# Software-pipelining the context quantization (phase D) and splitting the output rows (phase E) of a BitNet transformer layer on eight cores

## The chip, the cores and the metric

The kernel runs on the 8 cores of one Trainium2 chip, with the same program on every core and no communication between them. The metric is the device time of the slowest core in microseconds. Cores 0 to 3 form one die, 4 to 7 the other.

## The reference, cut to what matters

The input x is 4 x 4096 x 2048 in float32. The layer returns the input plus an attention branch plus a gated FFN branch, both fed with a layer-normalized x. All four projections of the attention are "bitlinear": ternary weights, and activations rounded to 8 bits with one scale for each token.

```python
def bitlinear(x, W):
    sw = jnp.mean(jnp.abs(W)) + 1e-05
    Wq = jnp.clip(jnp.round(W / sw), -1.0, 1.0) * sw
    sx = 127.0 / jnp.clip(jnp.max(jnp.abs(x), axis=-1, keepdims=True), 1e-05, None)
    xq = jnp.clip(jnp.round(x * sx), -128.0, 127.0) / sx
    return jnp.einsum('bsd,od->bso', xq, Wq)
...
p = jax.nn.softmax(scores, axis=-1)
out = jnp.einsum('bkgst,bktd->bkgsd', p, v)
out = out.transpose(...).reshape(b, s, D_MODEL)
return bitlinear(out, Wo)
...
x = x + attn(layernorm(x)) + ffn(layernorm(x))
```

The change touches the last two steps: the rounding of the attention's output (`out`, the context) ahead of `Wo`, and the product with `Wo` with the two additions.

## The kernel before, in words

A core owns 2048 tokens of one batch entry and goes through six parts, one after the other: the FFN for its tokens (its result goes to a DRAM scratch, `ffn_scr`), keys and values, queries, attention (phase C), **phase D**, the context's quantization, and **phase E**, the output projection. A `phase_fence` between parts makes every engine wait until PE, DVE and ACT have finished the part before.

Each `E(engine, fn, waits, inc)` appends one step to an engine's own program. Every engine runs its list in order. The waits are semaphore counts: `ve`, `pe` and `ac` count the steps of VectorE, TensorE and ScalarE, so a wait on `(ve, ve.n)` is a wait for the last VectorE step written so far, whatever it was. The order of the work is thus the order in which the code is written.

**Phase D** (L821 to L873) handles 16 tiles of 128 tokens, all in one chain of dependences. Attention left the context as `ctxT`, feature on the partitions. For a tile: TensorE transposes 8 blocks into a bank of the PSUM tile `d_ptr` and VectorE copies it to `ctok` (L840, L844), twice; VectorE multiplies by the inverse softmax sums into the float32 tile `d_cn` (L852), takes the row maximum (L855), and forms the scale and its inverse in two short steps (L858, L861); ScalarE scales and adds a large constant (L863) and subtracts it again with an integer output `d_ci` (L866), which rounds; VectorE casts to bf16 `d_cq` (L868); and `emit_tr16` (L190) transposes back in two groups of 8 through the same two banks of `d_ptr` (L198), each copied to `cqT` by VectorE (L202). Both kinds of transposes wait on `(ve, ve.n)`, and there is one `d_cn`, so one tile's chain ends before the next one's begins.

**Phase E** (L877 to L935) first quantizes `Wo` (`emit_wquant`: every weight chunk is loaded twice by SP's queue), and then for each of 16 token tiles SP's queue loads the 1 MB row block `e_x` of x (L896), POOL's queue loads the 1 MB block `e_f` of `ffn_scr` (L903), TensorE makes four groups of 16 matmuls of 512 columns (L910), alternating between two PSUM tiles `e_po`, ScalarE writes each group scaled into a quarter of `e_o` (L915), VectorE adds `e_x` (L920) and then `e_f` (L922) over all 2048 columns, and SP's queue stores the 1 MB block (L925). `e_x`, `e_f` and `e_o` have two buffers each. A load into a buffer waits for the additions two tiles earlier; but SP issues in order, so the load of `e_x` for a tile also stands behind the store of the tile before it. The program ends when the last stores have landed.

Of the kernel before, what the change touches and what calls it, by code (L numbers as in the profile page):

```python
# [44 lines left out]
def build_program():  # L45
# [49 lines left out]
    s_ost = [sem("s_ost0"), sem("s_ost1")]  # L95
# [724 lines left out]
    def phase_d():  # L820
        dstack = ExitStack()  # L821
        with dstack:
            ctok = sb("d_ctok", [128, D], BF16, dstack)
            cn = sb("d_cn", [128, D], F32, dstack)
            cm = cn
# [10 lines left out]
            for tt in range(16):  # L836
                for g in range(2):
# [23 lines left out]
                E("vector", lambda e, tt=tt: e.reciprocal(sx[:], rsxo[:, tt:tt + 1]),  # L861
                  waits=[(ve, ve.n)], inc=(ve, 1))
                E("scalar", lambda e: e.activation(cm[:], cn[:], AF.Identity,  # L863
                                                   scale=sx[:, 0:1], bias=bC1),
                  waits=[(ve, ve.n), (ac, ac.n)], inc=(ac, 1))
# [13 lines left out]
    def phase_e():  # L879
        estack = ExitStack()  # L880
        with estack:
# [10 lines left out]
            orow_st = [0, 0]  # L892
            efence = [(ve, ve.n), (ac, ac.n), (pe, pe.n)]
            for tt in range(16):
# [12 lines left out]
                for oc in range(4):  # L907
                    pb = oc % 2
                    E("tensor", lambda e, tt=tt, oc=oc, pb=pb: [
# [5 lines left out]
                    E("scalar", lambda e, tt=tt, oc=oc, pb=pb, tb=tb: e.activation(  # L915
                        orow[tb][:, oc * 512:(oc + 1) * 512], po[pb][:],
                        AF.Identity, scale=rsxo[:, tt:tt + 1]),
                      waits=[(pe, pe.n), (ac, ac.n), (s_ost[tb], orow_st[tb])], inc=(ac, 1))
# [9 lines left out]
                orow_st[tb] = s_ost[tb].n  # L928
            E("sync", None, waits=[(s_ost[0], s_ost[0].n), (s_ost[1], s_ost[1].n)])
# [118 lines left out]
```

How the kernel before makes its waits and increments, by code:

```python
            def _run(eng):  # L937
                for waits, fn, inc in prog.ops[name]:
                    for (s, v) in waits:
                        eng.wait_ge(s.h, v)
                    if fn is None:
                        continue
                    ins = fn(eng)
                    if inc is not None:
                        ins.then_inc(inc[0].h, inc[1])
```

## Time and profile before

| what | us |
|---|---|
| median of 2 runs (5829.81 and 5950.91) | 5890.36 |
| the profiled execution's own time | 5866.16 |
| its span, slowest core (core 6), first to last instruction | 5864.6 |
| span of the fastest core (core 3) | 5784.6 |
| granted TensorE clock, cores 0 to 3 / 4 to 7 | 0.848 / 0.841 |

The profile is one execution; start times count from the first instruction of core 6. A timeline row gives the start, the duration, the engine, the line, output <- input, and in brackets how long the engine was idle before and what released it. PE is TensorE, PEld its weight load, DVE is VectorE, ACT is ScalarE, POOL is GpSimd and SP is SyncE; SPq is a DMA issued by SP. A granted clock of 1.0 is 2.4 GHz and 0.5 is 1.2 GHz.

### The profile page before, as it was taken

What the parts mean: (1) busy time and instruction counts of PE and PEld (TensorE: products, weight loads), DVE (VectorE), ACT (ScalarE), POOL (GpSimd) and SP (SyncE); (2) the same over time, 40 slices, a digit from 0 to 9 for tenths busy, and PEclk for the clock granted to TensorE, in tenths of its full rate; (3) what the DMA queues carried; (4) which work ended last, traced back from release to release, by engine and by line L of the source; (5) the groups of instructions that cost most, each with busy time, mean ns of one, the idle gap of its engine ahead of it and who ended that gap; (6) DMA issues with size and microseconds to landing.
All of it is one profiled execution on the core that took longest, in us unless ns stands there. A gap on an engine that the chain in (4) does not pass through costs nothing.

```text
span 5864.6 us, 54466 instructions; the slowest of 8 cores (5784.6 to 5864.6 us)
## 1 busy us (share of the span) xinstructions
PE 3912.3 (67%) x18728; PEld 1781.8 (30%) x18728; DVE 1676.7 (29%) x2621; ACT 1638.0 (28%) x1375; POOL 303.0 (5%) x276
## 2 busy tenths in 40 slices
PE   1899978889998885244542044456889889922059
PEld 1344434434443442122331033342222222211024
DVE  4100000000000001455554365564322111144433
ACT  4111100011111001333330522213556656612131
POOL 0111110011111000000000000000000000000000
PEclk9999999999987997576776577789999999955579
DMA  3688877767766675311114501111000000000655
GB/s 117 65 79 75 77 69 81 81 72 72 72 63 63 72 84 101 111 58 49 51 49 115 147 31 44 44 33 46 11 9 8 7 5 6 4 0 0 165 194 215
DMA packets 793288, 387.59 MB, mean 66 GB/s; under 512 B 551488, under 2 KB 777152, under 8 KB 778688
## 3 DMA queue, kind: packets, MB, share of 16 engines
q0 software_dynamic: 548608, 161.50, 26.4%
q1 hardware_dynamic: 244416, 222.61, 12.9%
q8 instruction: 161, 2.64, 0.2%
q14 instruction: 103, 0.84, 0.1%
HBM read 480.53 MB, written 41.94 MB: 89 GB/s over the span
## 4 chain that ended last, share of the span: by engine, by line
PE 57%; DVE 18%; ACT 10%; DMA 9%; issue 5%; DVEq 1%; ACTq 0%; SPq 0%; POOL 0%; POOLq 0%
PE f_pd_h L341 11%; PE f_pg_h L300 11%; PE f_pu_h L306 11%; PE e_po L910 4%; PE c_pse L736 3%; PE c_ppv L740 3%; ACT c_pp L794 2%; DMA wo_wb<-wo_t 2%; PE c_psc L785 2%; DMA wq_wb<-wq_t 2%; PE c_psc L783 2%; PE c_pse L738 2%; PE c_ppv L742 2%; PE b_pkv L554 2%; DVE b_mx L165 2%
## 5 line engine op out<-in xcount | busy, mean ns | idle before, releaser
L794 ACT ACTIVATE c_pp<-c_psc 128x1024 bf16<-128x1024 f32 x640 | 655.4, 1024 | 581.4 <-PE c_psc L785 581.4
L300 PE MATMUL f_pg_h<-xnT,f_gw_h 128*128 128x512 bf16 x2816 | 655.1, 393 | 34.4 <-DMA f_uw_h<-uw_t 34.4
L341 PE MATMUL f_pd_h<-hdnT,f_dw_h 128*128 128x512 bf16 x2816 | 641.9, 391 | 44.5 <-DMA f_dw_h<-dw_t 44.5
L306 PE MATMUL f_pu_h<-xnT,f_uw_h 128*128 128x512 bf16 x2816 | 652.1, 392 | 0.0
L651 PE MATMUL b_pq<-b_xqT,qtern 128*128 128x256 bf16 x2048 | 270.3, 292 | 267.4 <-DVE b_qrot L660 258.7
L803 DVE TENSOR_TENSOR c_pp<-c_pp,cmask 128x512 bf16<-128x512 bf16 x512 | 217.8, 425 | 797.9 <-ACT c_pp L794 768.8
L321 DVE TENSOR_TENSOR hdnT<-f_sg_h,f_su_h 128x1024 bf16<-128x1024 bf16 x88 | 60.9, 693 | 1254.6 <-ACT f_su_h L317 1254.6
L341 PEld LDWEIGHTS f_pd_h<-hdnT,f_dw_h 128*128 128x128 bf16 x2816 | 283.9, 101 | 392.9 <-issue 83.3
L300 PEld LDWEIGHTS f_pg_h<-xnT,f_gw_h 128*128 128x128 bf16 x2816 | 282.8, 101 | 392.4 <-issue 133.3
L306 PEld LDWEIGHTS f_pu_h<-xnT,f_uw_h 128*128 128x128 bf16 x2816 | 282.6, 100 | 354.7 <-issue 97.2
L532 PE MATMUL b_pkv<-b_xqT,ktern 128*128 128x256 bf16 x1024 | 178.8, 357 | 288.4 <-DVE b_krot L541 271.5
L736 PE MATMUL c_pse<-c_pp,c_onehot 128*16 128x512 bf16 x640 | 244.8, 383 | 134.4 <-DVE c_pp L803 129.7
L651 PEld LDWEIGHTS b_pq<-b_xqT,qtern 128*128 128x128 bf16 x2048 | 206.2, 104 | 331.5 <-issue 295.2
L198 PE MATMUL b_ptr<-c_identbf,b_xq 128*128 128x128 bf16 x768 | 79.6, 286 | 327.9 <-DVE b_xq L187 327.9
L910 PE MATMUL e_po<-otern,cqT 128*128 128x512 bf16 x1024 | 224.0, 382 | 96.7 <-DVE otern L441 96.7
L358 DVE COPY f_ffs_h<-f_ptf_h 128x512 f32<-128x512 f32 x64 | 44.3, 692 | 766.8 <-PE f_ptf_h L354 766.8
L783 PE MATMUL c_psc<-c_qh,kT 128*128 128x512 bf16 x640 | 244.7, 382 | 21.3 <-DMA c_qh<-q_scr 21.3
L313 ACT ACTIVATE f_sg_h<-f_pg_h,c_gs 128x1024 bf16<-128x1024 f32 x88 | 98.1, 1115 | 557.6 <-PE f_pg_h L300 557.6
L740 PE MATMUL c_ppv<-c_pp,vT 128*128 128x512 bf16 x640 | 250.6, 392 | 0.0
L347 ACT ACTIVATE f_fft_h<-f_pd_h,c_ds 128x1024 f32<-128x1024 f32 x32 | 35.7, 1114 | 769.2 <-PE f_pd_h L341 769.2
L317 ACT ACTIVATE f_su_h<-f_pu_h,c_us 128x1024 bf16<-128x1024 f32 x88 | 98.1, 1115 | 538.2 <-PE f_pu_h L306 538.2
L785 PE MATMUL c_psc<-c_qh,kT 128*128 128x512 bf16 x640 | 245.0, 383 | 0.0
(163 smaller groups left out, 3996.8 us busy)
## 6 DMA issues: line engine op xcount, KB each, us to landing
f_gw_h<-gw_t POOLq DMA_DIRECT2D x88, 512.0 KB, 8.1
f_uw_h<-uw_t POOLq DMA_DIRECT2D x88, 512.0 KB, 10.1
f_dw_h<-dw_t POOLq DMA_DIRECT2D x32, 1408.0 KB, 18.0
b_xch<-x_kv SPq DMA_DIRECT2D x16, 2048.0 KB, 7.8
wq_wb<-wq_t SPq DMA_DIRECT2D x32, 1024.0 KB, 6.8
wo_wb<-wo_t SPq DMA_DIRECT2D x32, 1024.0 KB, 7.3
f_xch<-x_q SPq DMA_DIRECT2D x4, 4096.0 KB, 17.2
ffn_scr<-f_ffs_h SPq DMA_DIRECT2D x32, 512.0 KB, 11.3
```

The lines of the kernel that those rows point to most:

```text
L300: e.matmul(pg[:, bi, tc * 512:(tc + 1) * 512], gwb[bi][:, dt, :], xnT[:, dt, half * HT + tc * 512: half * HT + (tc + 1) * 512], start=(dt ...
L306: e.matmul(pu[:, bi, tc * 512:(tc + 1) * 512], uwb[bi][:, dt, :], xnT[:, dt, half * HT + tc * 512: half * HT + (tc + 1) * 512], start=(dt ...
L341: e.matmul(pd[:, bi, tc * 512:(tc + 1) * 512], dwb[bi][:, it, :], hdnT[:, it, tc * 512:(tc + 1) * 512], start=(it == 0), stop=(it == NIT - 1))
L532: e.matmul(pkv[pb][:, 0:256], ktern[:, dt, kv * 128:(kv + 1) * 128], xqT[:, cb, dt, :], start=(dt == 0), stop=(dt == NDT - 1))
L651: e.matmul(pq[pb][:], qtern[:, dt, h * 128:(h + 1) * 128], xqT[:, 0, dt, :], start=(dt == 0), stop=(dt == NDT - 1))
L736: e.matmul(pse[:], c_onehot[:, 16 * h:16 * h + 16], pp[:, k0 % 8, :], start=fse, stop=False),
L740: e.matmul(ppv[h % 2][:], vT[:, k0, kvh * 128:(kvh + 1) * 128], pp[:, k0 % 8, :], start=fpv, stop=False),
L783: e.matmul(psc[sbk][:, 0:512], kT[:, kvh, k0 * 128:(k0 + 1) * 128], qh[hb][:], start=True, stop=True),
L785: e.matmul(psc[sbk][:, 512:1024], kT[:, kvh, k1 * 128:(k1 + 1) * 128], qh[hb][:], start=True, stop=True)][-1],
L794: E("scalar", lambda e, k0=k0, sbk=sbk: e.activation(pp[:, (k0 % 8):(k0 % 8) + 2, :].rearrange("p a b -> p (a b)"), psc[sbk][:], AF.Exp, s ...
L803: E("vector", lambda e, k=k, mi=mi: e.tensor_mul(pp[:, k % 8, :], pp[:, k % 8, :], cmask[:, mi, :]), waits=[(ac, ac.n), MASKOK, (ve, ve.n) ...
L910: e.matmul(po[pb][:], cqT[:, dt, tt * 128:(tt + 1) * 128], otern[:, dt, oc * 512:(oc + 1) * 512], start=(dt == 0), stop=(dt == NDT - 1))
```

## The change

In phase D the loop body is cut into four functions. `stage_a` is the transposes, the copies to `ctok` and the multiplication; `stage_b` the maximum and the scales; `stage_c` the two ScalarE steps; `stage_d` the cast, the transposes back and the copies to `cqT`. The code writes `stage_c(tt)`, `stage_a(tt+1)`, `stage_b(tt+1)`, `stage_d(tt)`. `d_cn` and the inverse scale get two buffers, the transposes back get two PSUM banks of their own (`d_ptr2`), and the waits name the step that is really needed instead of the last one written, except for `stage_c`, which still waits on `(ve, ve.n)`: when it is written, that is the last copy of `stage_d(tt-1)`. In phase E the two additions and the store are done for each quarter of 512 columns, right behind the ScalarE step that made it, each quarter with its own store semaphore.

```diff
@@ phase_d
-            cn = sb("d_cn", [128, D], F32, dstack)
-            cm = cn
+            cn = sb("d_cn", [128, 2, D], F32, dstack)
...
-            sx = sb("d_sx", [128, 1], F32, dstack)
+            sx = sb("d_sx", [128, 2], F32, dstack)
...
+            ptr2 = ps("d_ptr2", [128, 2, 1024], BF16, dstack)
...
+            aptr_ve = [ve.n, ve.n]
+            cptr_ve = [ve.n, ve.n]
+            cn_ac = [ac.n, ac.n]
+            cq_ve = [ve.n]
+            p2_ac = [ac.n] * 16
+
+            def stage_a(tt):
+                tp = tt % 2
                 for g in range(2):
...
-                      waits=[(ve, ve.n)], inc=(pe, 1))
+                      waits=[(ve, aptr_ve[g])], inc=(pe, 1))
                     E("vector", lambda e, g=g, bank=bank: e.tensor_copy(
                         ctok[:, g * 1024:(g + 1) * 1024], bank[:]),
                       waits=[(pe, pe.n), (ve, ve.n)], inc=(ve, 1))
-
-                def bc_mul(e, tt=tt):
+                    aptr_ve[g] = ve.n
+
+                def bc_mul(e, tt=tt, tp=tp):
...
-                E("vector", bc_mul, waits=[(ve, ve.n), RSEOK], inc=(ve, 1))
...
+                E("vector", bc_mul, waits=[(ve, ve.n), RSEOK, (ac, cn_ac[tp])], inc=(ve, 1))
+
+            def stage_b(tt):
...
+            def stage_c(tt):
+                tp = tt % 2
+                E("scalar", lambda e, tp=tp: e.activation(cn[:, tp, :], cn[:, tp, :], AF.Identity,
+                                                          scale=sx[:, tp:tp + 1], bias=bC1),
                   waits=[(ve, ve.n), (ac, ac.n)], inc=(ac, 1))
...
+                  waits=[(ac, ac.n), (ve, cq_ve[0])], inc=(ac, 1))
+                cn_ac[tp] = ac.n
+                p2_ac[tt] = ac.n
+
+            def stage_d(tt):
                 E("vector", lambda e: e.tensor_scalar(cq[:], ci[:], 1.0, None, ALU.mult),
-                  waits=[(ac, ac.n), (pe, pe.n)], inc=(ve, 1))
+                  waits=[(ac, p2_ac[tt]), (pe, pipe_pe[0])], inc=(ve, 1))
...
-                          ptr, rdy, tt)
+                          ptr2, rdy, tt, cptr_ve)
+                pipe_pe[0] = pe.n
+
+            pipe_pe = [pe.n]
+            stage_a(0)
+            stage_b(0)
+            for tt in range(16):
+                stage_c(tt)
+                if tt + 1 < 16:
+                    stage_a(tt + 1)
+                    stage_b(tt + 1)
+                stage_d(tt)
@@ phase_e
...
-                      waits=[(pe, pe.n), (ac, ac.n), (s_ost[tb], orow_st[tb])], inc=(ac, 1))
+                      waits=[(pe, pe.n), (ac, ac.n), (s_ost[tb][oc], ost_oc[tb][oc])], inc=(ac, 1))
                     po_ac[pb] = ac.n
-                E("vector", lambda e, tb=tb: e.tensor_add(orow[tb][:], orow[tb][:], xrow[tb][:]),
-                  waits=[(ac, ac.n), XOK, (ve, ve.n)], inc=(ve, 1))
-                E("vector", lambda e, tb=tb: e.tensor_add(orow[tb][:], orow[tb][:], frow[tb][:]),
-                  waits=[(ve, ve.n), FROK], inc=(ve, 1))
+                    E("vector", lambda e, tb=tb, sl=sl: e.tensor_add(
+                        orow[tb][:, sl], orow[tb][:, sl], xrow[tb][:, sl]),
+                      waits=[(ac, ac.n), XOK, (ve, ve.n)], inc=(ve, 1))
+                    E("vector", lambda e, tb=tb, sl=sl: e.tensor_add(
+                        orow[tb][:, sl], orow[tb][:, sl], frow[tb][:, sl]),
+                      waits=[(ve, ve.n), FROK], inc=(ve, 1))
+                    E("sync", lambda e, tt=tt, tb=tb, sl=sl: e.dma_start(
+                        out=out[tt * 128:(tt + 1) * 128, sl], in_=orow[tb][:, sl]),
+                      waits=[(ve, ve.n)], inc=(s_ost[tb][oc], 16))
+                    ost_oc[tb][oc] = s_ost[tb][oc].n
                 row_ve[tb] = ve.n
-                E("sync", lambda e, tt=tt, tb=tb: e.dma_start(
-                    out=out[tt * 128:(tt + 1) * 128, :], in_=orow[tb][:]),
-                  waits=[(ve, ve.n)], inc=(s_ost[tb], 16))
```

VectorE in phase D, before, one tile in the steady state; the names in brackets are the engines' counters that the step waits for:

```order
L852 TENSOR_TENSOR d_cn<-d_ctok,d_rse 128x2048 [waits ve]
L855 TENSOR_REDUCE d_mx<-d_cn 128x1 [waits ve]
L858 TENSOR_SCALAR rsxo<-d_mx 128x1 [waits ve]
L861 RECIPROCAL d_sx<-rsxo 128x1 [waits ve]
L868 TENSOR_SCALAR d_cq<-d_ci 128x2048 [waits ac,pe]
L202 COPY cqT<-d_ptr 128x8x128 [waits pe] x2
L844 COPY d_ctok<-d_ptr 128x1024 [waits pe,ve] x2
```

VectorE at the same place, changed:

```order
L860 TENSOR_TENSOR d_cn<-d_ctok,d_rse 128x2048 [waits ve,ac]
L866 TENSOR_REDUCE d_mx<-d_cn 128x1 [waits ve]
L869 TENSOR_SCALAR rsxo<-d_mx 128x1 [waits ve]
L872 RECIPROCAL d_sx<-rsxo 128x1 [waits ve]
L888 TENSOR_SCALAR d_cq<-d_ci 128x2048 [waits ac,pe]
L202 COPY cqT<-d_ptr 128x8x128 [waits pe] x2
L851 COPY d_ctok<-d_ptr 128x1024 [waits pe,ve] x2
```

The steady rows read alike but belong to other tiles: the cast L888 now stands behind the scales of the next tile, so ScalarE's two steps have seven VectorE steps beside them. On TensorE, the start of phase D, changed (the rows x7 are the rest of a group of 8):

```order
L847 MATMUL d_ptr<-c_identbf,ctxT 128x128 [waits pe,ve,ac]
L847 MATMUL d_ptr<-c_identbf,ctxT 128x128 x7
L847 MATMUL d_ptr<-c_identbf,ctxT 128x128 [waits ve]
L847 MATMUL d_ptr<-c_identbf,ctxT 128x128 x7
L847 MATMUL d_ptr<-c_identbf,ctxT 128x128 [waits ve]
L847 MATMUL d_ptr<-c_identbf,ctxT 128x128 x7
L847 MATMUL d_ptr<-c_identbf,ctxT 128x128 [waits ve]
L847 MATMUL d_ptr<-c_identbf,ctxT 128x128 x7
L198 MATMUL d_ptr<-c_identbf,d_cq 128x128 [waits ve]
L198 MATMUL d_ptr<-c_identbf,d_cq 128x128 x7
```

The forward transposes of tile tt+1 now stand ahead of the transposes back of tile tt, so TensorE has four groups of 8 in a row: the two back (tile tt) and the two forward (tile tt+2). On SP's queue in phase E, changed (before, each tile had one store L925 of 128x2048 between two loads L896):

```order
L959 DMA out<-e_o 128x512 [waits ve] x4
L928 DMA e_x<-x_q 128x2048 [waits ve]
L959 DMA out<-e_o 128x512 [waits ve] x4
L928 DMA e_x<-x_q 128x2048 [waits ve]
L959 DMA out<-e_o 128x512 [waits ve] x4
```

The load of a tile still stands behind all stores of the tile before it.

## Rows read from the trace of the kernel before

**Rows 1.** The page's first line.
```profile
span 5864.6 us, 54466 instructions; the slowest of 8 cores (5784.6 to 5864.6 us)
```

**Rows 2.** Chain of waits, 5000 to 5865 us; below: start, us, what.
```profile
by line: PE e_po L910 25.9%; DMA wo_wb<-wo_t 13.5%; issue 4.5%; DVE d_cn L852 4.3%; DVE d_mx L855 4.3%; ACT d_cn L863 3.9%; PE d_ptr L198 3.8%; PE d_ptr L840 3.8%; ACT d_ci L866 3.7%; PE c_pse L736 2.7%; PE c_ppv L740 2.6%; DVE cqT L202 2.6
...
5630.46 224.06 PE e_po L910 x1024
```

**Rows 3.** Timeline of one tile of phase D: start, us, instruction [idle before <- releaser].
```profile
5158.35 0.69 DVE L844 COPY d_ctok<-d_ptr 128x1024 bf16<-128x1024 bf16 x1 [1.33 <-PE d_ptr L840]
...
5161.23 2.29 DVE L852 TENSOR_TENSOR d_cn<-d_ctok,d_rse 128x2048 f32<-128x2048 bf16 x1 [0.17 <-DVE d_ctok L844]
5163.63 2.29 DVE L855 TENSOR_REDUCE d_mx<-d_cn 128x1 f32<-128x2048 f32 x1
5166.02 0.15 DVE L858 TENSOR_SCALAR rsxo<-d_mx 128x1 f32<-128x1 f32 x1
5166.28 0.16 DVE L861 RECIPROCAL d_sx<-rsxo 128x1 f32<-128x1 f32 x1
5166.59 2.09 ACT L863 ACTIVATE d_cn<-d_cn,c_consts,d_sx 128x2048 f32<-128x2048 f32 x1 [15.00 <-DVE d_sx L861]
5168.78 2.00 ACT L866 ACTIVATE d_ci<-d_cn,c_consts 128x2048 int32<-128x2048 f32 x1
5170.95 1.23 DVE L868 TENSOR_SCALAR d_cq<-d_ci 128x2048 bf16<-128x2048 int32 x1 [4.51 <-ACT d_ci L866]
...
5173.55 0.69 DVE L202 COPY cqT<-d_ptr 128x1024 bf16<-128x1024 bf16 x1 [1.37 <-PE d_ptr L198]
...
5177.53 0.69 DVE L844 COPY d_ctok<-d_ptr 128x1024 bf16<-128x1024 bf16 x1 [1.33 <-PE d_ptr L840]
```

**Rows 4.** Timeline, first transposes and last copy of phase D.
```profile
5137.98 1.01 PE L840 MATMUL d_ptr<-c_identbf,ctxT 128*128 128x128 bf16 x8 [2.49 <-DVE d_rse L832]
...
5444.79 0.69 DVE L202 COPY cqT<-d_ptr 128x1024 bf16<-128x1024 bf16 x1 [1.26 <-PE d_ptr L198]
```

**Rows 5.** Windows: stretch, length, busy of PE, PEld, DVE, ACT, POOL; clock, DMA share, GB/s.
```profile
2425.00:2475.00 50.00, 18.71 (x107) 13.28 (x108) 26.64 (x42) 30.23 (x21) 0.00 (x0) 0.56 0.12 42
...
5128.00:5446.00 318.00, 67.87 (x524) 50.59 (x524) 147.38 (x155) 66.36 (x33) 0.00 (x0) 0.51 0.00 0
```

**Rows 6.** Timeline of the K/V projection: two transpose groups in a row.
```profile
2435.02 1.86 PE L198 MATMUL b_ptr<-c_identbf,b_xq 128*128 128x128 bf16 x16 [63.91 <-DVE b_xq L187]
...
2435.87 2.00 ACT L176 ACTIVATE b_xi<-b_xn,c_consts 128x2048 int32<-128x2048 f32 x1
2436.14 0.69 DVE L202 COPY b_xqT<-b_ptr 128x1024 bf16<-128x1024 bf16 x1 [1.37 <-PE b_ptr L198]
2436.99 0.69 DVE L202 COPY b_xqT<-b_ptr 128x1024 bf16<-128x1024 bf16 x1 [0.16 <-PE b_ptr L198]
```

**Rows 7.** Timeline, end of the program, ScalarE, VectorE and SP.
```profile
5854.71 0.69 ACT L915 ACTIVATE e_o<-e_po,rsxo 128x512 f32<-128x512 f32 x1 [2.77 <-PE e_po L910]
5855.64 2.29 DVE L920 TENSOR_TENSOR e_o<-e_o,e_x 128x2048 f32<-128x2048 f32 x1 [9.05 <-ACT e_o L915]
5858.10 2.29 DVE L922 TENSOR_TENSOR e_o<-e_o,e_f 128x2048 f32<-128x2048 f32 x1 [0.17 <-DVE e_o L920]
5860.47 0.34 SPq L925 DMA_DIRECT2D out<-e_o  x1
```

**Rows 8.** SP's wait at the end: us in total, times, longest us.
```profile
SPq L940 <- DMA out<-e_o: 3.4, 1, 3.4
```

**Rows 9.** Tile e_x: DVE's idle time before its adds, then landing of its loads.
```profile
  DMA e_x<-x_q: 64.4, 7
...
DMA to landing us min/median/max: 5.1/7.5/11.2
```

**Rows 10.** DMA issues: KB each, median us to landing (a small store).
```profile
q_scr<-b_qbf SPq DMA_DIRECT2D x128, 64.0 KB, 1.6
```

**Rows 11.** DVE groups by form: count, busy us, mean ns, idle before.
```profile
L655 DVE TENSOR_TENSOR b_q<-b_pq,ccqs 128x256 f32<-128x256 f32 x128 | 54.4, 425 | 19.2 <-PE b_pq L651 4.1 <-DVE b_sx L171 1.7 <-DVE b_qbf L665 0.8
```

More of the change, by code:

```diff
@@ L94, in build_program @@
     s_fr = [sem("s_fr0"), sem("s_fr1")]
-    s_ost = [sem("s_ost0"), sem("s_ost1")]
+    s_ost = [[sem(f"s_ost{i}_{j}") for j in range(4)] for i in range(2)]
     def sb(name, shape, dt, stack=None, side=None):
@@ L860, in phase_d @@
                   waits=[(ve, ve.n)], inc=(ve, 1))
-                E("vector", lambda e, tt=tt: e.reciprocal(sx[:], rsxo[:, tt:tt + 1]),
+                E("vector", lambda e, tt=tt, tp=tp: e.reciprocal(sx[:, tp:tp + 1],
+                                                                 rsxo[:, tt:tt + 1]),
                   waits=[(ve, ve.n)], inc=(ve, 1))
-                E("scalar", lambda e: e.activation(cm[:], cn[:], AF.Identity,
-                                                   scale=sx[:, 0:1], bias=bC1),
+            def stage_c(tt):
+                tp = tt % 2
+                E("scalar", lambda e, tp=tp: e.activation(cn[:, tp, :], cn[:, tp, :], AF.Identity,
+                                                          scale=sx[:, tp:tp + 1], bias=bC1),
                   waits=[(ve, ve.n), (ac, ac.n)], inc=(ac, 1))
-                E("scalar", lambda e: e.activation(ci[:], cm[:], AF.Identity, bias=bmC1),
-                  waits=[(ac, ac.n)], inc=(ac, 1))
+                E("scalar", lambda e, tp=tp: e.activation(ci[:], cn[:, tp, :], AF.Identity,
+                                                          bias=bmC1),
+                  waits=[(ac, ac.n), (ve, cq_ve[0])], inc=(ac, 1))
+                cn_ac[tp] = ac.n
+                p2_ac[tt] = ac.n
+            def stage_d(tt):
                 E("vector", lambda e: e.tensor_scalar(cq[:], ci[:], 1.0, None, ALU.mult),
-                  waits=[(ac, ac.n), (pe, pe.n)], inc=(ve, 1))
+                  waits=[(ac, p2_ac[tt]), (pe, pipe_pe[0])], inc=(ve, 1))
+                cq_ve[0] = ve.n
                 rdy = (ve, ve.n)
@@ L908, in phase_e @@
                     pb = oc % 2
+                    sl = slice(oc * 512, (oc + 1) * 512)
                     E("tensor", lambda e, tt=tt, oc=oc, pb=pb: [
@@ L914, in phase_e @@
                       waits=[(ac, po_ac[pb]), OTOK], inc=(pe, 1))
[L915 to L916 removed]
+                    E("scalar", lambda e, tt=tt, pb=pb, tb=tb, sl=sl: e.activation(
+                        orow[tb][:, sl], po[pb][:],
                         AF.Identity, scale=rsxo[:, tt:tt + 1]),
[L918 removed]
+                      waits=[(pe, pe.n), (ac, ac.n), (s_ost[tb][oc], ost_oc[tb][oc])], inc=(ac, 1))
                     po_ac[pb] = ac.n
[L920 to L929 removed]
+                    E("vector", lambda e, tb=tb, sl=sl: e.tensor_add(
[8 more added lines that the diff above has]
+                    ost_oc[tb][oc] = s_ost[tb][oc].n
+                row_ve[tb] = ve.n
+            E("sync", None, waits=[(s_ost[i][j], s_ost[i][j].n)
+                                   for i in range(2) for j in range(4)])
     phase_e()
```

11 lines of the change are left out of this document (5 added, 6 removed).

## The prediction, made before the changed kernel had run

> **What bounds the kernel now.** I read the first line of the page, then the chain of waits over the last part, then the timeline of one tile of phase D, then that of the end. The slowest core's span is 5864.6 us [rows 1] in an execution of 5866.2 us, so 1.6 us lie around it. In the last 865 us of the chain [rows 2] two things are to be seen: phase E is a single piece of 224.06 us of matmuls, so TensorE bounds it, and phase D is not one engine but VectorE, ScalarE and TensorE in turns. The timeline shows the turns [rows 3]: a tile takes 19.18 us (the first copy at 5158.35, the next tile's at 5177.53). VectorE sits idle 4.51 us for ScalarE and four times about 1.3 us for a transpose group (1.33 and 1.37 here, 1.26 in [rows 4], and one alike). So VectorE's own work is only some 9.4 us of 19.2. The windows agree: DVE is busy 147.38 us in 318, no DMA runs, and the granted clock of TensorE is 0.51, that is 1.2 GHz [rows 5]. Phase D lasts from 5137.98 to 5444.79 + 0.69 = 5445.48 [rows 4], 307.5 us, every bit of it on the path, since phase E starts behind a fence.
>
> **Phase D, the new cycle.** Take the end of the cast of one tile as 0. TensorE now has four groups of 8 transposes in a row: two back for this tile, two forward for a later one, each with a free bank. The K/V projection shows what two groups in a row cost [rows 6]: 16 transposes take 1.86 us where 8 take 1.01 [rows 4], so a further group adds 0.85 us; the first copy starts 1.37 us after VectorE's step before, and the second only 0.16 us behind the first, so copies start 0.85 us apart. Four copies start at 1.37, 2.22, 3.07 and 3.92 and the last ends at 4.61. From the start of the multiplication to the end of the reciprocal is 5166.28 + 0.16 - 5161.23 = 5.21 us [rows 3]. With the 0.17 us ahead of it: 4.61 + 0.17 + 5.21 = 9.99. The cast follows after a step of about 0.11 (as between L858 and L861) and takes 1.23: the cycle is 11.33 us in place of 19.18.
>
> Does ScalarE hide? Its two steps wait for VectorE's last step written so far, the second copy of the tile before, which ends at 2.91. They take 5168.78 + 2.00 - 5166.59 = 4.19 us [rows 3] and end at about 7.25; the cast needs them at 10.1. The cover is 2.8 us; if it were gone each microsecond beyond it would cost 15. Do the two engines slow each other? In the K/V projection ScalarE's rounding step takes 2.00 us with both copies beside it at 0.69 [rows 6], the same as alone in phase D. I cost that at nothing. The second buffers and banks cost only memory.
>
> **Phase D, the sum.** Filling: first copy 1.18 us after the first transpose (1.01 and one hand-over; the two around a group are 1.33 - 1.01 = 0.32 together, so I take 0.17), second 0.85 later, ending at 2.72; then 0.17 + 5.21 gives 8.10. The next tile's transposes are done by then: two copies of 0.69 with steps of 0.12 and 0.17 end at 9.77, and 0.17 + 5.21 + 0.11 + 1.23 ends its scales and the first cast at 16.5. Then 14 cycles: 158.6, to 175.1. Draining: copies to +2.91, ScalarE bare with 0.14 + 4.19, cast 0.17 + 1.23, copies 2.91, ends at 186.7. Gain: 307.5 - 186.7 = **120.8 us**. If each of the eight hand-overs in the cycle cost 0.1 us more than I read, the cycle would be 12.1 and the gain 109; nothing that I see makes it better than 11.33 but the clock (below).
>
> **Phase E, the end.** From the last ScalarE step (ends 5854.71 + 0.69 = 5855.40) VectorE starts 0.24 us later and needs 2.29 + 0.17 + 2.29 = 4.75 us [rows 7]. An addition of 512 columns is not in the trace. 256 float32 columns take 0.425 us [rows 11] and 2048 take 2.293, so one column costs (2293 - 425)/1792 = 1.042 ns and 512 take 0.69 us. A pair is 0.69 + 0.17 + 0.69 = 1.55 us: 3.2 us saved. The last store is 256 KB in place of 1 MB. The 1 MB store took 0.34 + 3.4 = 3.74 us from issue to the end of the wait [rows 7, 8]; the nearest small store is 64 KB in 1.6 us [rows 10]. 256 KB between them gives 2.0 us, 1.7 saved (bounds 0 and 2.1). End: **4.9 us**.
>
> **Phase E, the loop.** Here the change can cost. VectorE's additions rise from 4.75 us for a tile to four pairs of 1.72 us (with the step between pairs), 6.9 us, and the load of e_x, still behind all stores of the tile before on SP's queue, is now needed by the first quarter, not after the fourth. Behind a late load stand on VectorE the eight additions of the tile, behind them the stores, and behind these the next e_x load and POOL's e_f load. A tile of matmuls is 4 x (0.69 + 2.77) = 13.8 us, from ScalarE's row [rows 7]. The e_x load is issued 0.24 + 1.55 + 0.08 + 0.34 + 0.1 = 2.3 us after the last quarter (start, pair, step, issue of the store, step); three pairs (5.16) must be done 13.8 + 0.24 after it: no lag grows while the load lands within L = 14.06 - 5.16 - 2.3 = 6.6 us. Now it takes 5.1 to 11.2, median 7.5, and 7 of 16 times VectorE already waited for it, 64.4 us in total [rows 9], without TensorE ever waiting. But now a whole 1 MB store stands just ahead of it on its queue, beside a 1 MB e_f load; with 256 KB ahead instead, 2.25 MB move in place of 3, and I estimate 7.5 x 2.25/3 = 5.6 us. I take that: cost 0. With the median unchanged it is (7.5 - 6.6) x 15 = 13.5 us. TensorE itself is held only if VectorE falls a whole tile behind.
>
> **The sum.** 5866.2 - 120.8 - 4.9 = 5740.5, say **5740 us**, 2.14% less. The median of the two runs shown lies 24 us above the profiled execution, the lower run 36 below.
>
> **Rivals.**
> *TensorE's clock rises in phase D.* The granted clock was 0.51 there with PE busy 67.87 us in 318; in the K/V stretch with 18.71 in 50 it was 0.56 [rows 5]. The new cycle puts some 3.6 us of transposes in one piece into 11.3 us, 32% and near that stretch, so it might come up at times. Groups would take half: the first copy comes 0.43 us sooner and the others are then bound by VectorE at 0.69 + 0.16. That is 0.43 x 16 = 7 us: 5733. Against it: most of the K/V stretch, as busy, was at 1.2 GHz still. The Trainium skill (TensorE: Matmul & The Clock Gate, Part 1: The HAM clock gate) has it that the slow clock is the default and that sustained activity releases it, in two steps and nothing between. By that rule denser bursts are where a release would come; the mixed 0.56 agrees with a clock that switches.
>
> *Phase E becomes bound by the e_x chain.* It serializes load, eight additions and store. For it: 7 waits of 16 now, and a need that comes 10 us earlier in the tile. Against it: less traffic ahead, and tiles with a fast load catch up. With the landing at 7.5 us: 5740 + 13.5 = 5754. With every landing at the 11.2 of the slowest: (11.2 - 6.6) x 15 = 69, 5809.
>
> *Slower than before*, the same place: 125.7 us are given back if the chain is 8.4 us longer than the matmuls for each of 15 tiles, that is from L = 15.0 us. At twice the present median, also 15.0, it stands at 5866; at 16 it is 5881. That would take stores in 2 KB rows (four times as many pieces as now) to clog the queue. The slowest of 16 landings today, 11.2, speaks against it.
>
> *The overlap doesn't come about.* ScalarE's first step waits on the last VectorE step, not on the scale. Were it written after stage A and B, its 4.2 us and two steps would stand bare: cycle 15.8, gain 120.8 - 15 x 4.5 = 53, time 5808. The order of the rows on VectorE (the copies back, then the scales of the next tile, then the cast) speaks against it.
>
> **How the numbers follow.** The forecast (cycle near 11.3, no lag in E) 0.62; clock 0.10; e_x chain 0.24, mostly at its low end; slower 0.02; no overlap 0.02. Range: low end the clock's 5733 less the 36 us by which the lowest run lies under the profile, 5697; high end the chain at a lag of two thirds of its bound, 5740 + 46 = 5786, or the 5754 with the median's 24 and the dearer cycle's 12, 5790. I give 5697 to 5795. Faster by over 2%, about what a measurement of this kernel can tell from no change, needs a gain of 117 us; I have 125.7, so I count three quarters of the forecast, most of the clock's case and a fifth of the chain's: 0.60. Slower by over 2%: 0.01. The rest, 0.39, is within.
>
> **What would show it.** In the timeline of phase D: casts 11.3 us apart, ScalarE waiting for a copy to cqT and not for the reciprocal, VectorE without idle time ahead of the cast, one idle time of 1.37 us and three of about 0.16 before the four copies, phase D 187 us long. Clock still 0.5. In phase E: additions of 0.69 us, e_x landing at about 5.6 us, and TensorE in one piece of 224 us; the last addition 1.8 us after ScalarE's last step. I am wrong if the casts are over 12 us apart, if waits of e_x push the end more than 3 us behind TensorE, or if the store pieces slow the loads.

## The result, and the profile after

| | before | changed |
|---|---|---|
| median over all runs, us | 5846.59 (10 runs) | 5893.97 (11 runs) |
| lowest, us | 5813.03 | 5703.48 |
| profiled execution, us | 5866.16 | 5738.72 |
| span of its slowest core, us | 5864.6 (core 6) | 5737.1 (core 5) |

The ratio of the changed kernel to the kernel before is **0.9816, 95% interval 0.9762 to 0.9869**: 1.8% faster, and the interval lies on both sides of 2%. The medians over all runs point the other way only because in several runs the TensorE clock of a whole die was held down, with either kernel; the ratio leaves such runs out.

The page's first line and the chain of waits over the last part of the changed kernel (they answer to [rows 1, 2]):

```profile
span 5737.1 us, 54936 instructions; the slowest of 8 cores (5674.0 to 5737.1 us)
```

```profile
by line: DMA wo_wb<-wo_t 15.9%; DMA e_x<-x_q 15.9%; DVE e_o L956 5.8%; DVE e_o L953 5.8%; issue 5.5%; DVE d_cn L860 5.0%; DVE d_mx L866 5.0%; PE d_ptr L198 4.0%; PE d_ptr L847 2.9%; DVE d_cq L888 2.7%; PE c_pse L736 2.6%; PE c_ppv L740 2.6%
```

Before, phase E was one piece of 224 us of matmuls in this chain. Now the matmuls `e_po` are not even among the first twelve: in their place stand the loads of `e_x` and VectorE's additions. The bound of phase E has changed hands.

The timeline of phase D, one cycle of the changed kernel (it answers to [rows 3]):

```profile
5176.38 1.23 DVE L888 TENSOR_SCALAR d_cq<-d_ci 128x2048 bf16<-128x2048 int32 x1
...
5178.97 0.69 DVE L202 COPY cqT<-d_ptr 128x1024 bf16<-128x1024 bf16 x1 [1.37 <-PE d_ptr L198]
...
5179.83 0.69 DVE L202 COPY cqT<-d_ptr 128x1024 bf16<-128x1024 bf16 x1 [0.16 <-PE d_ptr L198]
5180.67 2.10 ACT L878 ACTIVATE d_cn<-d_cn,c_consts,d_sx 128x2048 f32<-128x2048 f32 x1 [7.13 <-DVE cqT L202]
5180.75 0.69 DVE L851 COPY d_ctok<-d_ptr 128x1024 bf16<-128x1024 bf16 x1 [0.23 <-PE d_ptr L847]
5181.60 0.69 DVE L851 COPY d_ctok<-d_ptr 128x1024 bf16<-128x1024 bf16 x1 [0.16 <-DVE d_ctok L851]
5182.53 2.29 DVE L860 TENSOR_TENSOR d_cn<-d_ctok,d_rse 128x2048 f32<-128x2048 bf16 x1 [0.24 <-DVE d_ctok L851]
5182.91 2.00 ACT L881 ACTIVATE d_ci<-d_cn,c_consts 128x2048 int32<-128x2048 f32 x1
...
5187.75 1.23 DVE L888 TENSOR_SCALAR d_cq<-d_ci 128x2048 bf16<-128x2048 int32 x1
```

The casts are 5187.75 - 5176.38 = 11.37 us apart. One idle time of 1.37 us is left ahead of the copies, the other three are 0.16 to 0.23, and the cast has no bracket at all: in the steady state VectorE doesn't wait for ScalarE. Phase D, first transpose to last copy, takes 188.2 us on core 5 (187.9 to 188.2 on the others) in place of 307.4 to 307.6.

Phase E near the end, in the same timeline (it answers to [rows 7]):

```profile
5707.73 0.38 SPq L928 DMA_DIRECT2D e_x<-x_q  x1
...
5714.09 0.69 DVE L953 TENSOR_TENSOR e_o<-e_o,e_x 128x512 f32<-128x512 f32 x1 [6.85 <-DMA e_x<-x_q]
...
5716.34 0.69 ACT L948 ACTIVATE e_o<-e_po,rsxo 128x512 f32<-128x512 f32 x1 [2.76 <-PE e_po L943]
...
5721.13 0.38 SPq L928 DMA_DIRECT2D e_x<-x_q  x1
5727.43 0.69 DVE L953 TENSOR_TENSOR e_o<-e_o,e_x 128x512 f32<-128x512 f32 x1 [6.80 <-DMA e_x<-x_q]
...
5733.28 0.69 DVE L956 TENSOR_TENSOR e_o<-e_o,e_f 128x512 f32<-128x512 f32 x1 [0.17 <-DVE e_o L953]
```

ScalarE, and TensorE with it, ends at 5716.34 + 0.69 = 5717.0. The last tile's `e_x` is issued only 4 us after that, and the last addition ends at 5734.0, **17.0 us behind ScalarE**. Before it was 5.0 (5.5 and 6.3 on two other cores). This distance is called the lag from here on. The tile's own rows, `e_x` in the changed kernel (idle time of VectorE before its additions, and the loads' landing; they answer to [rows 9]), and SP's wait at the end (to [rows 8]):

```profile
  DMA e_x<-x_q: 134.4, 16
...
DMA to landing us min/median/max: 6.0/7.1/11.0
```

```profile
SPq L976 <- DMA out<-e_o: 1.8, 1, 1.8
```

VectorE waits for `e_x` in all 16 tiles, 134.4 us, in place of 7 times and 64.4. The landing is 7.1 us in the median, hardly under the 7.5 of before, and the mean of the 16 loads is 7.7 in both.

**Where the time went**, slowest core against slowest core:

| stretch | before, core 6 | changed, core 5 | difference |
|---|---|---|---|
| start of the program to phase D (first `d_rse` step) | 5136.1 | 5113.4 | -22.7 |
| phase D | 307.50 | 188.15 | -119.35 |
| quantizing `Wo` | 185.0 | 186.0 | +1.0 |
| phase E, first matmul to last addition | 229.9 | 244.5 | +14.6 |
| last addition to the end of the span | 4.2 | 3.1 | -1.1 |

(Between the first two rows lie 1.9 us in both kernels.) The phases from D on give -104.8 us, 1.8% of 5866, which is what the ratio says. The first row has nothing to do with the change: phase D starts anywhere from 5059 to 5136 us on the eight cores of the kernel before. That these two executions differ by 127 us in all is partly luck.

### The profile page after: what moved, and what is told of

Its sections match the earlier page's. It is cut to its first block, busy times and chain, and to the rows that moved or that the text cites. A ratio compares the mean times of both kernels' runs of the same rounds, so it can differ in the third digit from the quotient of the medians.

```text
span 5737.1 us, 54936 instructions; the slowest of 8 cores (5674.0 to 5737.1 us)
## 1 busy us (share of the span) xinstructions
PE 3874.1 (68%) x18728; PEld 1777.7 (31%) x18728; DVE 1692.0 (29%) x2717; ACT 1640.2 (29%) x1375; POOL 303.0 (5%) x276
## 3 DMA queue, kind: packets, MB, share of 16 engines
q1 hardware_dynamic: 251328, 222.61, 13.5%
## 4 chain that ended last, share of the span: by engine, by line
PE 54%; DVE 20%; DMA 11%; ACT 9%; issue 5%; DVEq 1%; SPq 0%; ACTq 0%; POOLq 0%; POOL 0%
PE f_pd_h L341 11%; PE f_pg_h L300 11%; PE f_pu_h L306 11%; PE c_pse L736 3%; PE c_ppv L740 3%; ACT c_pp L794 2%; DMA wo_wb<-wo_t 2%; DMA e_x<-x_q 2%; DMA wq_wb<-wq_t 2%; PE c_psc L785 2%; PE c_psc L783 2%; PE b_pkv L554 2%; PE c_ppv L742 2%; PE c_pse L738 2%; DVE b_mx L165 2%
## 5 line engine op out<-in xcount | busy, mean ns | idle before, releaser
L300 PE MATMUL f_pg_h<-xnT,f_gw_h 128*128 128x512 bf16 x2816 | 640.7, 387 | 31.9 <-DMA f_uw_h<-uw_t 31.9
L306 PE MATMUL f_pu_h<-xnT,f_uw_h 128*128 128x512 bf16 x2816 | 637.1, 385 | 0.0
L736 PE MATMUL c_pse<-c_pp,c_onehot 128*16 128x512 bf16 x640 | 244.7, 382 | 134.4 <-DVE c_pp L803 129.7
L785 PE MATMUL c_psc<-c_qh,kT 128*128 128x512 bf16 x640 | 244.5, 382 | 0.0
## 6 DMA issues: line engine op xcount, KB each, us to landing
ffn_scr<-f_ffs_h SPq DMA_DIRECT2D x32, 512.0 KB, 11.2
```

The costliest lines, as they stand in the source:

```text
L300: e.matmul(pg[:, bi, tc * 512:(tc + 1) * 512], gwb[bi][:, dt, :], xnT[:, dt, half * HT + tc * 512: half * HT + (tc + 1) * 512], start=(dt ...
L306: e.matmul(pu[:, bi, tc * 512:(tc + 1) * 512], uwb[bi][:, dt, :], xnT[:, dt, half * HT + tc * 512: half * HT + (tc + 1) * 512], start=(dt ...
L736: e.matmul(pse[:], c_onehot[:, 16 * h:16 * h + 16], pp[:, k0 % 8, :], start=fse, stop=False),
L785: e.matmul(psc[sbk][:, 512:1024], kT[:, kvh, k1 * 128:(k1 + 1) * 128], qh[hb][:], start=True, stop=True)][-1],
```

## The experiments

Lengths of phases, landings and the lag are read from the traces of all cores; the lag is the end of the last addition less the end of ScalarE's last step, at the end of the program or, where it is said, of one tile.

**Which part does what: phase D alone, phase E alone.** `d_only` has the changed `phase_d` and the old `phase_e`; `e_only` has the old `phase_d` and the changed `phase_e`.

> The changed phase D with the old phase E. If the gain is all in phase D and the changed phase E costs (theory: e_x lands too late for the first quarter), phase D lasts 188 us, phase E from its first matmul to its last addition 230 us as before, and the whole is 120 us under the kernel before (ratio 0.979), some 13 us better than the full change. Rival: phase E's additional time in the changed kernel comes from the shorter phase D (stages of the cores meeting differently at the memory), then phase E is about 245 us here too.

> The old phase D with the changed phase E. Theory: phase E lasts 245 us in place of 230 where TensorE's clock is full, with 14 to 16 waits for e_x and the last addition 17 us behind ScalarE's last step; the whole is 10 to 13 us slower than before (ratio 1.002). Rival (as forecast: landing at 5.6 us): last addition 1.8 us behind ScalarE and the whole 5 us faster (0.999).

`d_only`: ratio 0.9804 (0.9641 to 0.9967). Phase D is 187.9 to 188.1 us on every core, the median core's phase E 230.1 us (229.0 to 236.2). `e_only`: ratio 1.0022 (0.9969 to 1.0075), phase D 307.4 to 307.6, phase E 236.3 to 244.9 us on seven cores, lag 11.9 to 20.2. On the eighth, core 6, phase E took 259.7 us: its loads landed at 9.0 us in the median, the lag rose to 27.6 us within the phase, and then ScalarE waited 63.5 us in all for stores, with TensorE waiting behind it. Both totals came out as the first theory has them, but their intervals alone don't separate it from the rival; the phase lengths do. The cost in phase E belongs to the change in phase E and appears with the long phase D too. A surprise in `d_only`: with the old phase E the lag was 5.0 on four cores and 7.0 to 10.8 on the others, and `e_x` landed at 7.5 to 8.1 in the median. The kernel before shows it too: on its six cores with the full clock the lag rose to between 7.9 and 9.9 us within the phase, and on four of them it was back at 5.0 at the end. The old loop already stood at its edge.

**Is it the late load?** `x_load(t)` issues the load of `e_x` for tile t, which stood at the head of the loop.

```diff
...
+            x_load(0)
+            x_load(1)
             for tt in range(16):
...
                 row_ve[tb] = ve.n
+                if tt + 2 < 16:
+                    x_load(tt + 2)
```

> The changed kernel with each e_x load issued one tile earlier: two up front, then tile tt+2 behind the stores of tile tt. Same loads, same stores, same additions. Theory (a late e_x is the whole cost in phase E): no waits for e_x after the first tile, last addition 1.8 us behind ScalarE, phase E 227 us, the whole 16 to 17 us under the changed kernel (ratio to before about 0.978 if that has 0.981). Rival (the eight additions of a tile and the small stores cost by themselves): phase E stays at 240 or more.

The ratio is 0.9807 (0.9686 to 0.9929), too wide to tell 17 us. The phase lengths do it: phase E lasted 225.0 to 226.8 us and the lag was 1.8 on all eight cores. Tile `e_x`, slowest core of `x_first`:

```profile
  ACT e_o L956: 112.5, 60
  DMA e_x<-x_q: 7.8, 1
...
DMA to landing us min/median/max: 6.1/6.8/12.8
```

One wait for `e_x` is left where there were 16, and 60 of 64 times VectorE now waits for ScalarE, that is for the matmuls. The same 64 small stores and 128 additions are there, and the load lands no sooner (medians of 6.6 to 7.5 us on the eight cores). So neither the stores nor the additions cost by themselves; what cost was where the load stood. Some 16 us of phase E come back.

**What sets the landing, which I had forecast at 5.6 us?** Three kernels. `one_store` keeps the additions by quarters and writes the row block in one store behind them:

```diff
-                    E("sync", ... out=out[tt * 128:(tt + 1) * 128, sl], in_=orow[tb][:, sl] ...)
+                E("sync", ... out=out[tt * 128:(tt + 1) * 128, :], in_=orow[tb][:] ...)
```

> The changed kernel with the additions by quarters but one 1 MB store for the four. My traffic estimate (7.5 us with 1 MB ahead of e_x, 5.6 with 256 KB) gives a landing of 7.5 us, longer than with small stores. Rival: what is ahead of e_x on the queue is the same either way since the four small stores follow each other 1.66 us apart and each needs about as long; then the landing stays at 7.1 to 7.5 and the lag at the end at 15 to 20 us. Second rival: rows of 2 KB move worse than rows of 8 KB; then e_x lands under 7 us here and the lag shrinks below 10.

Landing 7.5 us in the median on five cores (7.6 to 8.2 on the others), lag 14.9 to 15.4 on the six cores with a full or nearly full clock. ScalarE also waited for stores, 46.0 us on the slowest core against 25.5 in the changed kernel, since it needs the whole block stored before it may write the first quarter. The landing was foretold by two of the theories alike, so this kernel told little; it excludes that 2 KB rows are what makes it long.

`q3_only` issues the store only for the last quarter, so three quarters of the output stay unwritten, and `no_f` loads `e_f` for two tiles only, so most of the output lacks the FFN branch. In `q3_only` ScalarE also waits for the additions of two tiles before, in place of the stores that are gone; its tiles still take 13.8 us.

```diff
-                    E("sync", lambda e, tt=tt, tb=tb, sl=sl: e.dma_start(
+                    if oc == 3: E("sync", lambda e, tt=tt, tb=tb, sl=sl: e.dma_start(
```

```diff
-                E("gpsimd", lambda e, tt=tt, tb=tb: e.dma_start(
+                if tt < 2: E("gpsimd", lambda e, tt=tt, tb=tb: e.dma_start(
```

> The changed kernel with the store of the last quarter only (three quarters of the output are left out). Ahead of e_x on its queue there is then one 256 KB store and nothing older. Rival theory (own queue): landing falls to about 5.5 us, under the 6.6 us from which a lag grows, and the last addition comes 1.8 us behind ScalarE. Traffic estimate: 1.5 of 3 MB for each tile, also under 6. If it stays at 7 us with the lag, neither holds, and the load's time is set by memory shared with other cores or by a fixed delay.

> The changed kernel with e_f loaded for the first two tiles only (later tiles add stale rows: the FFN branch is left out of most of the output). My traffic estimate (landing in proportion to all that is in flight) gives 7.2 x 1.25/2.25 = 4.0 us for e_x and no lag. Rival (e_f's packets run behind those of e_x, as the packet times of the changed kernel show, and e_x waits for the stores ahead on its own queue): landing stays at 6.5 to 7.2 us and the lag at the end at 10 us or more.

Tile `e_x`, slowest core of each, `q3_only` first:

```profile
  DMA e_x<-x_q: 119.3, 15
...
DMA to landing us min/median/max: 5.8/6.9/9.7
```

```profile
  DMA e_x<-x_q: 99.7, 15
...
DMA to landing us min/median/max: 5.4/6.0/6.8
```

Both theories missed on the landing. Without three of four stores its median is still 6.5 to 7.1 on the eight cores and the lag 6.2 to 12.3. But the timeline shows that this edit took little away from ahead of the load: on core 5 of the changed kernel, where the last load is issued at 5721.13, the first two stores of the tile before have landed (5718.09 and 5719.72) and the third lands at 5721.45. The store directly ahead, landing at 5724.16, stays in `q3_only`. Without `e_f` the median landing is 5.8 to 6.4, with a maximum of 7.8: the traffic of `e_f` costs about 1 us and nearly all of the late landings, but nothing near the 3 us that my proportion gave (4.0).

The store directly ahead stood in all these kernels. It landed 4.8 us after its own issue where it is 1 MB (kernel before, `one_store`) and 3.6 to 3.7 where it is 256 KB, medians over the eight cores; the load landed 3.2 to 3.7 us after it (2.7 in `no_f`), and never before it. The first load of the phase, with no store ahead, landed after 4.8 to 7.1 us in the kernel before and 5.4 to 7.4 in the changed one. So the store ahead may well hold the load, its smaller size bringing about 1 us; a kernel without it wasn't run, and what the rest of the landing is made of stays open.

One thing was confirmed on the way: I had worked out that no lag grows while the landing is under 6.6 us. In `no_f`, with means of 5.9 to 6.4, the lag is 1.8 at the end on all eight cores (never over 3.5 within the phase) although VectorE still waits for `e_x` 13 to 16 times; in `q3_only`, with means of 6.7 to 7.2, it grows. Whether the late landings with `e_f` come from this core's own transfers or from those of its neighbours, which all lost theirs too, is open; I didn't try it.

**Phase D: is it the order that hides ScalarE?** `c_late` moves one call:

```diff
             for tt in range(16):
-                stage_c(tt)
                 if tt + 1 < 16:
                     stage_a(tt + 1)
                     stage_b(tt + 1)
+                stage_c(tt)
                 stage_d(tt)
```

> The changed kernel with stage_c written behind stage_a and stage_b of the next tile; nothing else moved. ScalarE's first step then waits for the next tile's reciprocal, and its 4.2 us stand bare before the cast. Theory (the order written decides, since the wait is on the last step written): the cycle rises from 11.37 to about 15.7 us and phase D from 188 to about 253 us. Rival (buffers and banks bring the gain, not the place of the wait): cycle under 12.

Phase D lasts 256.4 to 256.5 us. Timeline of `c_late`, one tile:

```profile
5201.78 0.16 DVE L872 RECIPROCAL d_sx<-rsxo 128x1 f32<-128x1 f32 x1
5202.09 2.09 ACT L878 ACTIVATE d_cn<-d_cn,c_consts,d_sx 128x2048 f32<-128x2048 f32 x1 [11.69 <-DVE d_sx L872]
5204.33 2.00 ACT L881 ACTIVATE d_ci<-d_cn,c_consts 128x2048 int32<-128x2048 f32 x1
5206.51 1.23 DVE L888 TENSOR_SCALAR d_cq<-d_ci 128x2048 bf16<-128x2048 int32 x1 [4.57 <-ACT d_ci L881]
...
5222.44 1.23 DVE L888 TENSOR_SCALAR d_cq<-d_ci 128x2048 bf16<-128x2048 int32 x1 [4.57 <-ACT d_ci L881]
```

ScalarE starts behind the wrong tile's reciprocal, the 4.57 us of idle time are back ahead of the cast, and the cycle is 15.93 us. All buffers and banks are as in the changed kernel; 68 of its 119 us are lost through the place of one line, since the wait takes the count of whatever was written last.

**How much cover does ScalarE have?** `act1` and `act2` add one and two ScalarE steps to each tile (n is 1 and 2).

```diff
                 cn_ac[tp] = ac.n
+                for _ in range(n):
+                    E("scalar", lambda e, tp=tp: e.activation(c_junk[:], cn[:, tp, :], AF.Identity,
+                                                              bias=bmC1),
+                      waits=[(ac, ac.n)], inc=(ac, 1))
+                cn_ac[tp] = ac.n
```

> The changed kernel with one more ScalarE step of 2.0 us in each tile (the rounding step written once more, into a tile that nobody reads). Theory: the cover over ScalarE is 2.8 us, so the cycle stays at 11.4 us and phase D grows by the one bare step at the end, to 190 us. Rival (ScalarE's chain is near the bound): cycle 13.4, phase D 218.

> The same with two such steps, 4.1 us. Theory: 1.4 us beyond the cover, the cycle rises to 12.8 us and phase D to about 213 us, with VectorE idle 1.4 us ahead of the cast in each tile. Rival: as for one step, cycle 15.4 and phase D 250.

With one step phase D is 190.0 to 190.2 us, with two 214.5. Timeline of `act2`:

```profile
5196.07 0.16 DVE L872 RECIPROCAL d_sx<-rsxo 128x1 f32<-128x1 f32 x1
5197.76 1.23 DVE L893 TENSOR_SCALAR d_cq<-d_ci 128x2048 bf16<-128x2048 int32 x1 [1.53 <-ACT c_junk L886]
```

2.0 us more of ScalarE cost nothing but the bare one at the end; 4.2 us (two steps of 2.0 and what lies between) show as 1.53 us ahead of each cast and a cycle of 12.89 us, 1.5 longer. The cover is thus about 2.7 us, where 2.8 was read.

**What are the separate banks worth?** `old_banks` puts the transposes back into the banks of `d_ptr` with the old waits:

```diff
-                          ptr2, rdy, tt, cptr_ve)
+                          ptr, rdy, tt)
...
-                      waits=[(ve, aptr_ve[g])], inc=(pe, 1))
+                      waits=[(ve, ve.n)], inc=(pe, 1))
```

> The changed kernel with all transposes of phase D back in the two banks of d_ptr and with the old waits on the last VectorE step; the order of the stages and the double d_cn stay. Theory: each of the four copies has a transpose group bare ahead of it again (three times 1.3 us in place of 0.16 to 0.23), so the cycle is 11.37 + 3.3 = 14.7 us and phase D 237 us. Rival (banks matter little, since a group takes only 1 us): cycle below 12.5.

Phase D is 241.3 us on every core. Timeline of `old_banks`, the copies of one tile:

```profile
5162.85 0.69 DVE L202 COPY cqT<-d_ptr 128x1024 bf16<-128x1024 bf16 x1 [1.37 <-PE d_ptr L198]
...
5164.81 0.69 DVE L202 COPY cqT<-d_ptr 128x1024 bf16<-128x1024 bf16 x1 [1.26 <-PE d_ptr L198]
...
5166.83 0.69 DVE L851 COPY d_ctok<-d_ptr 128x1024 bf16<-128x1024 bf16 x1 [1.33 <-PE d_ptr L847]
...
5168.85 0.69 DVE L851 COPY d_ctok<-d_ptr 128x1024 bf16<-128x1024 bf16 x1 [1.33 <-PE d_ptr L847]
```

Every copy has a bare transpose group ahead of it again, three of them more than in the changed kernel. 53 of the 119 us need the banks and their exact waits; the other 66 come with the rest: the order, the second `d_cn` and the exact waits that this kernel keeps.

**Was the old phase E better off without the quarters?** `b_xfirst` is the kernel before with the loads of `e_x` one tile earlier, the same edit as in `x_first`.

> The kernel before with e_x loaded one tile earlier; one store and whole-row additions as before. Theory (the old order had a little slack and hid the load): waits for e_x disappear or nearly so, last addition 5.0 us behind ScalarE on every core, phase E 229 to 230 us as before, so nothing is gained there; the division into quarters is then worth the 3.2 us between 5.0 and the 1.8 of x_first, and some 1.5 us of the shorter last store. Rival: phase E falls to 226 as well.

No waits for `e_x`, the lag 5.0 us on every core, phase E 228.8 to 229.8 us on the six cores with the full clock (272 on two whose matmuls ran slower). Nothing gained there, as the first theory has it; the quarters are worth 3.2 us of lag, but only with the earlier load.

**A version that is better.** `best` has the earlier load and multiplies straight from PSUM:

```diff
-                    E("vector", lambda e, g=g, bank=bank: e.tensor_copy(
-                        ctok[:, g * 1024:(g + 1) * 1024], bank[:]),
-                      waits=[(pe, pe.n), (ve, ve.n)], inc=(ve, 1))
...
+                    def bc_mul(e, tt=tt, tp=tp, g=g, bank=bank):
+                        a = bank.rearrange("p (h d) -> p h d", d=128)
+                        b = rse[:, tt, g * 8:(g + 1) * 8].rearrange("p (h o) -> p h o", o=1)
+                        a2, b2 = broadcast_tensor_aps(a, b)
+                        return e.tensor_tensor(
+                            cn[:, tp, g * 1024:(g + 1) * 1024].rearrange("p (h d) -> p h d", d=128),
+                            a2, b2, ALU.mult)
```

> The changed kernel with e_x loaded one tile earlier (as in x_first) and with the multiplication reading the transposed context straight from its PSUM bank, in two halves of 1024 columns, so that the copies to ctok are gone. Theory (VectorE's list is the cycle of phase D): two copies of 0.69 us and their steps go, the multiplication in two halves takes 2 x 1.23 + 0.17 in place of 2.29, so the cycle falls from 11.37 to about 10.0 us and phase D from 188 to 167; with phase E at 226 the whole is about 5660 us (ratio 0.974 to 0.976). Rival (a PSUM operand makes the two-input step slower, or ScalarE's cover of 2.8 us is used up): cycle stays over 11.

Ratio 0.977 (0.971 to 0.9829), lowest run 5673.15 us. Timeline of `best`:

```profile
5170.63 1.22 DVE L856 TENSOR_TENSOR d_cn<-d_ptr,d_rse 128x1024 f32<-128x1024 bf16 x1 [0.30 <-PE d_ptr L847]
5172.02 1.23 DVE L856 TENSOR_TENSOR d_cn<-d_ptr,d_rse 128x1024 f32<-128x1024 bf16 x1 [0.17 <-DVE d_cn L856]
...
5176.17 1.23 DVE L887 TENSOR_SCALAR d_cq<-d_ci 128x2048 bf16<-128x2048 int32 x1
...
5186.16 1.23 DVE L887 TENSOR_SCALAR d_cq<-d_ci 128x2048 bf16<-128x2048 int32 x1
```

The cycle is 9.99 us, phase D 165.2 to 165.3, and phase E 224.8 to 226.8 with a lag of 1.8. By its phases it is 23 + 17 = 40 us under the changed kernel. The intervals of the two ratios overlap, so that is shown by the phases, and the lowest runs agree (5673 against 5703); the ratio doesn't show it.

## Why the prediction was right, and where it was wrong

**Direction and size: right for phase D, wrong for phase E.** The forecast was 125.7 us; the phases give 104.8 and the ratio 108 (1.84% of 5866). Of the 20.9 us missing, 17.8 are phase E's loop, 1.4 phase D, 1.0 the quantizing of `Wo`, 0.6 the end. "Faster by over 2%" had 0.60; the 1.8% lie just short of it, and the interval decides neither way. That the profiled execution took 5738.7 us, almost the 5740 predicted, is a coincidence of two errors: 21 us too much gain, and an earlier part that happened to be 22.7 us shorter.

*Phase D, the new cycle (11.33 us).* Right: 11.37. Each piece came as read, the first copy at +1.37, the others 0.85 to 0.92 apart.

*ScalarE hides, with 2.8 us of cover.* Right (2.7), and tested at both sides with `act1` and `act2`. The rival without overlap was priced at a cycle of 15.8 us; made on purpose in `c_late`, it is 15.9.

*Phase D, the sum (120.8 us).* Right: 119.4. The first cast ended 16.5 us in, as worked out; the missing 1.4 us lie in the 14 cycles, whose mean is 11.43 since three of them are 0.2 to 0.4 us longer. I didn't look for the reason.

*The last store (1.7 us).* Nearly right: SP waited 1.8 us in place of 3.4, and from the last addition to the end it is 1.1 us less.

*The last additions (3.2 us saved).* Right as an amount, but it didn't come: it shows only where the lag is not set by the load. `x_first` has it, 1.8 in place of 5.0.

*Phase E, the loop (cost 0).* This is the step that failed, and by the prediction's own sign: waits of `e_x` were not to push the end over 3 us behind TensorE, and they pushed it 17. The mechanism was described as it is, down to L, the landing from which a lag grows. The same cycle of a tile in the kernel before, where a lag was tolerated longer:

```profile
5820.45 0.44 SPq L896 DMA_DIRECT2D e_x<-x_q  x1
...
5828.36 2.29 DVE L920 TENSOR_TENSOR e_o<-e_o,e_x 128x2048 f32<-128x2048 f32 x1 [8.42 <-DMA e_x<-x_q]
...
5833.63 0.39 SPq L896 DMA_DIRECT2D e_x<-x_q  x1
```

VectorE starts 0.16 us after the landing. From there to the next load's issue it is 5833.63 - 5828.36 = 5.3 us here and 5721.13 - 5714.09 = 7.0 in the changed kernel, since the eight short additions take 6.5 us where the two long ones took 4.75. Taken from a tile of 13.8 us, that leaves a landing of 8.4 us before and 6.6 now. Single tiles agree: loads of 9.0 and 11.2 us added 0.6 and 3.1 us to the lag before; loads of 9.2, 9.8, 10.3 and 11.0 us added 2.7, 3.5, 4.0 and 4.3 in the changed kernel. So the limit fell by 1.8 us, below the mean landing, which hardly moved: 7.75 and 7.73 us on these two cores, 8.0 and 7.4 over all eight.

What was wrong was the landing: "2.25 MB move in place of 3, and I estimate 7.5 x 2.25/3 = 5.6 us". Its median was 7.1 on the slowest core and 6.4 to 7.4 over the eight. The estimate scaled the whole time with the traffic, as if a transfer had no part of its own; but my own nearest small transfer, 64 KB in 1.6 us [rows 10], has hardly any bytes. Scaling only what lies above that, 1.6 + (7.5 - 1.6) x 2.25/3 gives 6.0, still too low. And pricing by the median was wrong too, since a lag adds up every load: (7.1 - 6.6) x 15 is 7.5 us, while the 15 loads behind the first have a mean of 7.84, which gives 18.6. Measured are 17.0 - 1.8 = 15.2 us of lag and 2.7 us by which TensorE was held (its matmuls span 226.7 us in place of 224.0), together the 17.8 us above but for rounding. The price for an unchanged median, 13.5 us, comes nearer, but by luck: the median did fall, and it was the mean that counted. The rival "phase E becomes bound by the e_x chain", with a chance of 0.24, is what happened, at its low end: 5754 by the prediction, and 5866.2 - 104.8 = 5761 by the phases.

The Trainium skill (DMA: Bandwidth & Descriptors, Anatomy of one DMA) gives a DMA on GpSimd's path about 2 us of fixed time beside a part in proportion to the bytes. The small store and `e_x` are issued by SP, so this carries over in kind only; the 1.6 us of the small store agree with that. As an estimate by the page's fit, a 1 MB load alone would take 4.4 us; the shortest landing of `e_x` here, with all cores at work, is 4.8 (kernel before, core 4).

*The clock (a rival at 0.10).* It does come up, and gives nothing. Windows of the changed kernel, core 5: the burst of four transpose groups, the rest of that cycle, and phase D from its second tile on (stretch, length, busy us of PE, PEld, DVE, ACT, POOL; clock, DMA share, GB/s; they answer to [rows 5]):

```profile
5177.80:5181.50 3.70, 3.57 (x32) 3.33 (x32) 2.08 (x3) 0.83 (x1) 0.00 (x0) 0.50 0.02 4
5181.50:5187.70 6.20, 0.00 (x0) 0.00 (x0) 5.54 (x5) 3.27 (x2) 0.00 (x0) 0.78 0.00 0
...
5125.00:5304.00 179.00, 53.62 (x480) 49.93 (x480) 134.63 (x137) 64.21 (x32) 0.00 (x0) 0.55 0.00 1
```

The clock is at 1.2 GHz all through the burst. In some cycles, as in this one, it is at 2.4 GHz for part of the time behind the burst, when TensorE has nothing to do; by the next burst it is down again. On the other cores it reaches into some bursts: 38 of 512 transposes on core 6, six on core 5. Over phase D the granted clock is 0.55 in place of 0.51. The 16 transposes still take 1.86 us, as in [rows 6], so the 7 us of that rival did not come; phase D is 187.9 us on core 6 and 188.2 on core 5.

## What to carry to other kernels

When the consumer of a load is moved earlier, for instance by cutting a step into pieces, look at when the load is issued, and work out how late it may land in both kernels; here 119 us won in one phase were partly given back, 15 us, in another because the load still stood behind the last piece's store. Issue loads by the buffer's freedom, not behind the previous result. And when each wait is a count of "the last step written so far", the order in which stages are written is a set of dependences: moving one call cost 68 us with the same buffers.

## What the runs showed that I had not expected

The old phase E was already at its edge: with the long phase D taken away but phase E unchanged (`d_only`), four of eight cores showed a lag of 7.0 to 10.8 us behind ScalarE where 5.0 is the least. Also, a slower TensorE lets the lag drain: on cores 6 and 7 of the changed kernel it had grown to about 11 us in tiles of 13.8 us, as elsewhere; then the granted clock fell (0.81 on core 6 from 5550 us on), a tile took 16.8 us, and the lag shrank by about 3 us a tile to 1.8. Their matmuls span 244.8 and 249.6 us, some 21 and 26 more than the 223 to 224 of most other cores, but their phase E is 247.5 and 252.3, only 5 and 10 us over the others' 242 in the median: such a core loses less in phase E than its matmuls alone say.
